# Four chained graph networks: edge ranks by units of 32 columns, and the empty slots filled ahead of the small loads

## The chip, the cores and the metric

The kernel runs on one core of one Trainium2 chip. The metric is the device time of one execution, in microseconds; of before there are three runs, and their median counts. Engines are named as in the profile: PE is TensorE (PEld its weight loads), DVE is VectorE, ACT is ScalarE, POOL is GpSimd, SP is SyncE, which here only issues DMAs.

## The reference, cut to what matters

Four graph networks run one after the other on the same graph of 6,250 nodes with 64 features and 200,000 edges (src, dst, a weight, 16 and 8 attributes). Each one reads rows of its node table at src, works on them, and sums them by dst:

```python
edge_index = jnp.stack([src, dst])
h = jnp.maximum(_layernorm(x, axis=-1), 0.0)
x = x + _L0_gnn_ref(h, L0_gnn_W, L0_gnn_b, edge_weight, src, dst)      # 3 layers: segment_sum(w * ht[col], row)
h = jnp.maximum(_layernorm(x, axis=-1), 0.0)
x = x + _L1_gnn_ref(h, edge_attr_16, ..., src, dst)                    # attention, softmax by dst
h = jnp.maximum(_layernorm(x, axis=-1), 0.0)
x = x + _L2_gnn_ref(h, edge_index, edge_attr_8, ...)                   # MLP on edges, segment_sum by dst
h = jnp.maximum(_layernorm(x, axis=-1), 0.0)
x = x + _L3_gnn_ref(h, src, dst, ...)                                  # attention, softmax by dst
```

The change touches none of these sums, but the sort of the edges that stands ahead of them.

## The kernel before, in words

The nodes are cut into 49 tiles of 128 (T), and the kernel first sorts the edges by the tile of their dst. There are NB = 50 bins, one per tile and one for padding. The edges lie as 128 partitions by KC = 1568 columns. The sort has these steps:

1. SP loads the constants and dst. DVE writes a template of empty slots into `fill`, and SP stores it 42 times (640 KB each) over `packed`, the table of sorted records in DRAM, so that slots which get no edge are harmless. Ahead of these stores SP issues 40 small loads of weights (`small_loads`), the group ids and X.
2. DVE and ACT count the edges of each bin per partition (`bucket` holds each edge's bin); PE makes prefix sums, and DVE turns them into `base`, the place of the first edge of each bin and partition, less one. DVE also makes a schedule of tiles, `sched_i`, which SP stores to DRAM and loads back.
3. DVE ranks the edges. For a group of columns and each bin it makes a mask, a running count that starts at `base`, the new carry, the count where the mask is one, and adds that to `rank`: five instructions per bin and group. The groups are `PLACED`, 2, 3, 5, 9, 15 and 15 units of 32 columns. After each group `rank` becomes the slot number `pos`, and `pos_made` is raised.
4. SP loads the edges' records (`slab`, from `payload`) and their positions (`slab_pos`) by halves of a unit, 16 columns each, into one of two buffers, when `pos_made` covers the group and the scatters that read the buffer have landed (`scattered`).
5. POOL scatters the records, one indirect DMA per column, 32 a unit and 1568 in all, to `packed`. It starts when all 42 fills have landed (`filled`), since they write the same table.

When the last scatter has landed, SP loads the sorted records piece by piece (UZ<-packed), DVE unpacks them, and the passes over the edges begin: gathers of table rows on POOL, one-hot matrices on DVE, sums on PE. While POOL scatters, DVE goes on after the ranks with work that doesn't need the records: `RES`, which marks the first group of each tile, the small weights, and the node work of the first layer (`layer_input`, `norm_to`, on X and U, which is half of UZ).

The helpers `tt`, `ts`, `stt` and `reduce64` wait for the engine's last instruction and issue tensor_tensor, tensor_scalar, scalar_tensor_tensor and a sum over the last axis. In the profile they appear under one line each, 481, 485, 489 and 477. Names that end in a digit lose it there: EA is EA8, in which bucket, rank, pos and others lie.

Of the kernel before, what the change touches and what calls it, by code (L numbers as in the profile page):

```python
# [19 lines left out]
ALU = mybir.AluOpType  # L20
# [3 lines left out]
P = 128  # L24
# [7 lines left out]
NB = T + 1  # L32
KC = -(-N_EDGES // (P * 32)) * 32
SLAB = 16
# [1 line left out]
BODY = 16  # L36
LAG = 8
NG = -(-((N_EDGES + T * (GE - 1)) // GE) // BODY) * BODY
PLACED = [2, 3, 5, 9, 15, 15]
ACT_BINS = 28  # L40
PACK = 40
NS = 1680
# [19 lines left out]
LN_EPS = 1e-5  # L62

assert STEPS_N % 2 == 1 and 2 * ITER * PIECE == 2 * NG
assert max(PLACED) * 2 * SLAB <= 512 and sum(PLACED) * 2 * SLAB == KC and NS % PACK == 0 and (NS // PACK) % 2 == 0 and KC % (2 * SLAB) == 0
assert NS * P >= NG * GE + P * KC - N_EDGES + GE and P * SCHED >= NG + BODY

# [32 lines left out]
def build(nc, d, out):  # L101
    with ExitStack() as ctx:
        def sb(name, shape, dt=F32):
            return ctx.enter_context(nc.sbuf_tensor(name, shape, dt))

        def sem(name):
            return ctx.enter_context(nc.semaphore(name))
# [3 lines left out]
        UZ = sb("UZ", [P, 2, TP, D])  # L111
# [15 lines left out]
        bucket, mask, signs, rank = (ea8_flat[:, i * KC:(i + 1) * KC] for i in range(4))  # L127
        signs = signs.bitcast(BF16).rearrange("p (h c) -> p h c", h=2)
        dst_raw = ea8_flat[:, 5 * KC:6 * KC].bitcast(I32)
        pos = ea8_flat[:, 6 * KC:7 * KC].bitcast(I32)  # L130
        pos_hi = ea8_flat[:, 7 * KC:8 * KC].bitcast(I32)
# [8 lines left out]
        fill = y_flat[:, 0:PACK * PAY].rearrange("p (s c) -> p s c", c=PAY)  # L140
        slab = y_flat[:, PACK * PAY:PACK * PAY + 2 * SLAB * PAY].rearrange("p (h s c) -> p h s c", h=2, c=PAY)
        slab_pos = sb("slab_pos", [P, 2, SLAB], I32)
        itmp = sb("itmp", [P, 2, PIECE], I32)
        prod16 = sb("prod16", [P, PIECE, D16])
        cnt, base, tot, grp, cum = (sb(n, [P, NB]) for n in ("cnt", "base", "tot", "grp", "cum"))
# [6 lines left out]

        const = sb("const", [P, C_ALL])
        ident, tri = const[:, C_ID:C_ID + P], const[:, C_TRI:C_TRI + P]
        iota, ones = const[:, C_IOTA:C_IOTA + P], const[:, C_ONE:C_ONE + P]
        bins, groups = const[:, C_BIN:C_BIN + NB], const[:, C_GRP:C_GRP + SCHED]
        pad_nodes = const[:, C_PAD:C_PAD + PAD_TILES]
# [72 lines left out]
        bank = [ctx.enter_context(nc.psum_tensor(f"bank{i}", [P, 512], F32)) for i in range(8)]  # L230
# [10 lines left out]
        packed = nc.dram_tensor("packed", (P, NS, PAY), F32).ap()  # L241
# [7 lines left out]
        fill_made, filled = sem("fill_made"), sem("filled")  # L249
# [1 line left out]
        counted, prefixes = sem("counted"), sem("prefixes")  # L251
        bucket_made, signs_summed = sem("bucket_made"), sem("signs_summed")
        sched_made, sched_stored, sched_loaded = sem("sched_made"), sem("sched_stored"), sem("sched_loaded")
        pos_made = sem("pos_made")
        slab_in = [sem("slab_in0"), sem("slab_in1")]
        scattered = [sem("scattered0"), sem("scattered1")]
        pack_in = [sem("pack_in0"), sem("pack_in1")]
# [53 lines left out]
        def ds(start, size):  # L311
            return slice(start, start + size) if isinstance(start, int) else bass.ds(start, size)
# [5 lines left out]
        def _(sp):  # L318
# [8 lines left out]
            for h in range(2):  # L327
                at = slice(h * D, (h + 1) * D)
# [7 lines left out]
                for k in range(h * D8, P, 2 * D8):  # L336
                    small_loads.append((we_f[k:k + D8, h, :], d["w2_1"][2 * D:2 * D + D8, :]))

            sp.wait_ge(fill_made, 1)
            for to, what in small_loads:  # L340
                sp.dma_start(to, what).then_inc(s_w, 16)
            sp.dma_start(gid, d["group_ids"]).then_inc(s_gid, 16)
            sp.dma_start(X[:, 0:T, :], d["x"]).then_inc(s_x, 16)

            sp.wait_ge(fill_made, 2)
            for k in range(NS // PACK):
                sp.dma_start(packed[:, k * PACK:(k + 1) * PACK, :], fill).then_inc(filled, 16)

            sp.wait_ge(sched_made, 2)
            sp.dma_start(sched_d.rearrange("(p j) -> p j", p=P), sched_i[:, :]).then_inc(sched_stored, 16)  # L350
# [4 lines left out]
            for h in range(2):  # L355
                sp.dma_start(slab[:, h, :, :], d["payload"][:, h * SLAB:(h + 1) * SLAB, :]).then_inc(slab_in[h], 16)
                sp.dma_start(slab_pos[:, h, :], pos[:, h * SLAB:(h + 1) * SLAB]).then_inc(slab_in[h], 16)
            for j in range(len(PLACED)):
                sp.wait_ge(pos_made, j + 1)
                with sp.Fori(max(sum(PLACED[:j]), 1), sum(PLACED[:j + 1])) as i:  # L360
                    for h in range(2):
                        sp.wait_ge(scattered[h], i * (16 * SLAB))
                        at = i * (2 * SLAB) + h * SLAB
                        sp.dma_start(slab[:, h, :, :], d["payload"][:, bass.ds(at, SLAB), :]).then_inc(slab_in[h], 16)
                        sp.dma_start(slab_pos[:, h, :], pos[:, bass.ds(at, SLAB)]).then_inc(slab_in[h], 16)

            for h in range(2):
                sp.wait_ge(scattered[h], KC // (2 * SLAB) * 16 * SLAB)
# [84 lines left out]
        def _(v):  # L453
            own = Own(v, dve_done)
# [20 lines left out]
            def reduce64(to, what):  # L475
                own.wait()
                own.count(v.tensor_reduce(to, what, AX.X, ALU.add))

            def tt(to, a, b, op):
                own.wait()  # L480
                own.count(v.tensor_tensor(to, a, b, op))

            def ts(to, a, s1, s2, op0, op1=ALU.bypass):
                own.wait()
                own.count(v.tensor_scalar(to, a, s1, s2, op0, op1))

            def stt(to, a, s, b, op0, op1):
                own.wait()
                own.count(v.scalar_tensor_tensor(to, a, s, b, op0, op1))
# [5 lines left out]
            def move(to, a):  # L495

                return v.tensor_scalar(to, a, 1.0, None, ALU.mult)  # L497
# [13 lines left out]
            v.memset(fill[:, :, DST_AT:DST_AT + 1].bitcast(I32), NO_DST).then_inc(fill_made, 1)  # L511
            own.count(v.memset(X[:, T:TP, :], 0.0))
            own.count(v.memset(sched[:, :], 0))
            own.count(v.memset(SRC[:, 2 * NG:], 0))
            own.count(v.memset(rank, 0.0))
            own.count(v.tensor_copy(iota_b[:, :], iota))
            own.count(v.tensor_copy(ident_b[:, :], ident))

# [8 lines left out]
            at0 = own.n  # L527
# [32 lines left out]
            v.memset(itmp[:, :, :], 0).then_inc(sched_made, 1)  # L560

            c1 = 0
            for units in PLACED:
                c0, c1 = c1, c1 + units * 2 * SLAB
                here = slice(c0, c1)
                ps_mask, ps_scan = bank[3][:, 0:c1 - c0], bank[4][:, 0:c1 - c0]
                at0 = own.n
                with v.Fori(0, NB) as b:
                    own.n = b * 5 + at0  # L570
                    one, carry = bins[:, bass.ds(b, 1)], base[:, bass.ds(b, 1)]
                    ts(ps_mask, bucket[:, here], one, None, ALU.is_equal)
                    own.wait()
                    own.count(v.tensor_tensor_scan(ps_scan, ones[:, 0:1].to_broadcast([P, c1 - c0]), ps_mask,
                                                   carry, ALU.mult, ALU.add))
                    own.wait()
                    own.count(move(carry, ps_scan[:, c1 - c0 - 1:c1 - c0]))
                    stt(ps_mask, bucket[:, here], one, ps_scan, ALU.is_equal, ALU.mult)
                    tt(rank[:, here], rank[:, here], ps_mask, ALU.add)
                own.n = at0 + 5 * NB  # L580
                own.wait()
                own.count(v.tensor_copy(pos[:, here], rank[:, here]))
                own.wait()
                own.count(v.tensor_scalar(pos_hi[:, here], pos[:, here], 7, None, ALU.logical_shift_right))
                own.wait()
                own.count(v.tensor_scalar(pos[:, here], pos[:, here], P - 1, None, ALU.bitwise_and))
                own.wait()
                v.scalar_tensor_tensor(pos[:, here], pos[:, here], float(NS), pos_hi[:, here],
                                       ALU.mult, ALU.add).then_inc(pos_made, 1)

            own.count(v.memset(RES[:, :], 0.0))
# [1 line left out]
            at0 = own.n  # L594
# [12 lines left out]
            for h in range(2):  # L607
                at = slice(h * D, (h + 1) * D)
# [12 lines left out]
            for k in range(3):  # L621
                at = slice(32 * k, 32 * k + 32)
                own.count(v.tensor_copy(WE[at, :], we_parts[at, k, :]))
            at = slice(96, P)
# [1052 lines left out]
```

## Time and profile before

| what | before |
| --- | --- |
| runs, us | 14564.51, 14566.06, 14582.17 |
| median | 14566.06 us |
| the profiled execution's own time | 14585.36 us |
| its span from first to last instruction | 14583.5 us |
| PE, DVE, POOL, ACT busy | 9509.5, 10155.7, 10612.6, 4114.1 us |
| first and last scatter of the sort, start | 157.3 and 2198.1 us |

Engines work side by side, so these busy times overlap. The first 2,200 us are the sort, and the rest the six passes over the edges. "Start" counts from the span's first instruction.

### The profile page before, as it was taken

To read this page: it belongs to the slowest core of one execution; us is meant where nothing else is said; L and a number is where in the kernel's file an instruction comes from. 1 tells how busy PE (TensorE), PEld (TensorE's weight loads), DVE (VectorE), ACT (ScalarE), POOL (GpSimd) and SP (SyncE) were. 2 spreads that over 40 slices of the span, in tenths; PEclk is the share of its full clock that TensorE was granted. 3 is DMA by queue.
4 is the path that set the end of the run, shared out by engine and by line. 5 is a ranking of instruction groups with operands and counts; after the bars stand their busy time and mean duration, and the time that the engine had idled before them with its cause. 6 is when DMAs were issued, how large, how long until landed. Compare 5 with 4: busy or idle time off the path is not lost.

```text
span 14583.5 us, 379790 instructions
## 1 busy us (share of the span) xinstructions
PE 9509.5 (65%) x89162; PEld 8547.0 (59%) x89163; DVE 10155.7 (70%) x46548; ACT 4114.1 (28%) x13780; POOL 10612.6 (73%) x10932
## 2 busy tenths in 40 slices
PE   0000006777778888788887888887555555788888
PEld 0000006777767777677776777777444444777777
DVE  7870007777776666666666888888766666888888
ACT  1000000000000000000000888887222222677777
POOL 3777777777767777677776777776677777677776
PEclk9995558888888888888888555555555555555555
DMA  2101112222211111111111111111111111111111
GB/s 100 27 25 26 26 26 48 41 42 41 38 27 26 27 27 27 27 27 27 27 27 26 28 28 27 27 27 23 28 26 26 27 27 26 28 27 27 27 27 29
DMA packets 499490, 443.36 MB, mean 30 GB/s; under 512 B 291533, under 2 KB 316749, under 8 KB 498254
## 3 DMA queue, kind: packets, MB, share of 16 engines
q0 software_dynamic: 349696, 337.89, 14.0%
q1 hardware_dynamic: 149454, 102.38, 2.5%
q14 instruction: 303, 2.48, 0.1%
q8 instruction: 37, 0.61, 0.0%
HBM read 368.39 MB, written 65.20 MB: 30 GB/s over the span
## 4 chain that ended last, share of the span: by engine, by line
PE 35%; issue 18%; DVE 17%; POOL 15%; DVEq 8%; DMA 6%; ACT 1%; POOLq 0%; ACTq 0%; SPq 0%
PE bank L1463 16%; PE bank L1438 11%; POOL packed L423 10%; POOL G L442 6%; DMA G<-table,idx 5%; DVEq L705 3%; PE bank L1520 3%; DVE OH L722 2%; PE bank L1532 2%; PE bank L1451 1%; PE bank L1509 1%; DVE OHB L733 1%; DVEq L707 1%; DVE OHT L761 1%; PE bank L1536 1%
## 5 line engine op out<-in xcount | busy, mean ns | idle before, releaser
L442 POOL DMA_INDIRECT G<-table,idx x9360 | 9084.3, 971 | 3264.8 <-issue 2412.9
L1463 PE MATMUL bank<-UZ,OHT 128*128 128x192 bf16 x15600 | 2086.4, 260 | 544.8 <-DVE OHT L761 544.8
L1438 PE MATMUL bank<-G,OH 128*128 128x64 f32 x9984 | 1686.3, 301 | 598.1 <-DVE OH L722 454.9
L423 POOL DMA_INDIRECT packed<-Y,slab_pos x1568 | 1528.1, 975 | 670.5 <-issue 494.7
L1356 ACT ACTIVATE OHB<-bank,const 128x512 bf16<-128x512 f32 x159 | 109.3, 688 | 6729.7 <-PE bank L1451 6729.7
L1463 PE MATMUL bank<-UZ,V 128*128 128x192 bf16 x14976 | 1992.8, 259 | 0.0
L1438 PEld LDWEIGHTS bank<-G,OH 128*128 128x128 f32 x9984 | 1496.1, 217 | 772.2 <-DVE OH L722 693.9
L1463 PEld LDWEIGHTS bank<-UZ,OHT 128*128 128x128 bf16 x15600 | 1505.8, 111 | 584.6 <-DVE OHT L761 563.1
L1438 PE MATMUL bank<-ZR,OH 128*128 128x65 f32 x6656 | 1765.6, 419 | 1.3 <-DVE ZR L829 1.3
L1438 PEld LDWEIGHTS bank<-ZR,OH 128*128 128x128 f32 x6656 | 1623.9, 334 | 1.9 <-DVE ZR L829 1.7
L722 DVE TENSOR_SCALAR OH<-const,DL,W 128x128 f32<-128x128 f32 x4992 | 1561.2, 368 | 0.2 <-issue 0.2
L761 DVE TENSOR_SCALAR OHT<-OHB 128x512 bf16<-128x512 bf16 x3900 | 1161.4, 298 | 388.5 <-issue 387.2
L866 DVE TENSOR_TENSOR ACC<-ACC,bank 128x64 f32 x2496 | 550.8, 221 | 1248.8 <-PE bank L1438 1206.3
L1463 PEld LDWEIGHTS bank<-UZ,V 128*128 128x128 bf16 x14976 | 1404.6, 104 | 16.0
L1532 PE MATMUL bank<-ER,OHT 128*128 x9984 | 959.8, 174 | 454.9 <-DVE negm_lo L807 265.9
L1520 PE MATMUL bank<-const,V 128*128 128x128 f32 x3328 | 1119.7, 440 | 147.4 <-ACT V L1322 145.4
L1532 PEld LDWEIGHTS bank<-ER,OHT 128*128 128x128 bf16 x9984 | 801.4, 109 | 702.8 <-issue 554.3
L761 DVE TENSOR_SCALAR V<-OHB 128x512 bf16<-128x512 bf16 x3744 | 1136.5, 304 | 0.0
L1451 PE MATMUL bank<-const,chosen 128*128 128x128 f32 x1272 | 220.8, 328 | 1297.6 <-DVE chosen L497 1297.6
L733 DVE TENSOR_TENSOR OHB<-iota_b,DLw 128x256 bf16<-128x256 bf16 x2496 | 1051.5, 421 | 21.3 <-issue 13.5
L1509 PE MATMUL bank<-ident_b,OHB 128*128 128x128 bf16 x4992 | 1009.3, 306 | 43.4 <-DVE OHB L733 43.4
L1451 PEld LDWEIGHTS bank<-const,chosen 128*128 128x128 f32 x1272 | 193.7, 231 | 1298.2 <-DVE chosen L497 1298.2
(281 smaller groups left out, 18632.0 us busy)
## 6 DMA issues: line engine op xcount, KB each, us to landing
G<-table,idx POOLq DMA_INDIRECT x9360, 2.5
packed<-Y SPq DMA_DIRECT2D x42, 640.0 KB, 17.4
UZ<-packed SPq DMA_DIRECT2D x104, 256.0 KB, 2.7
Y<-in_payload SPq DMA_DIRECT2D x98, 256.0 KB
packed<-Y,slab_pos POOLq DMA_INDIRECT x1568
table<-Y SPq DMA_DIRECT2D x6, 1690.0 KB, 5.5
idx<-SRC SPq DMA_DIRECT2D x624, 8.0 KB
X<-in_x SPq DMA_DIRECT2D x1, 1568.0 KB, 8.8
```

The costliest lines, as they stand in the source:

```text
L423: pool.indirect_dma_start(out=packed_rows, out_offset=bass.IndirectOffsetOnAxis(ap=slab_pos[:, h, c:c + 1], axis=0), in_=slab[:, h, c, :], ...
L442: pool.indirect_dma_start(out=G[:, 2 * q + c, :], out_offset=None, in_=table, in_offset=bass.IndirectOffsetOnAxis(ap=idx[:, h, j:j + 1], a ...
L722: o = v.tensor_scalar(OH[:, q, c, :], iota, DL[:, at], W[:, at], ALU.is_equal, ALU.mult)
L733: v.tensor_tensor(OHB[:, q, :, :], iota_b[:, :].unsqueeze(1).to_broadcast([P, 2, P]), DLw[:, 2 * u:2 * u + 2].unsqueeze(2).to_broadcast([P ...
L761: v.tensor_scalar(tile_hot(tile), code, float(tile), None, ALU.is_equal).then_inc(tile_ready, 1)
L866: v.tensor_tensor(acc, acc, ps_a[r % 2][:, 0:D], ALU.add).then_inc(acc_done, 1)
L1438: o = pe.matmul(ps_a[r % 2][:, 0:w], OH[:, q, c, :], parts[c], start=c == 0, stop=c == 1)
L1451: o = pe.matmul(ps_code[:, c * P:(c + 1) * P], chosen[:, c:c + 1].to_broadcast([P, P]), ident, start=True, stop=True)
L1463: o = pe.matmul(ps_rows[c // 2][:, c % 2 * 3 * D:(c % 2 + 1) * 3 * D], tile_hot(tile)[:, c * P:(c + 1) * P], table_parts[:, tile, :, :].re ...
L1509: o = pe.matmul(ps_m[r % 2][:, c * P:(c + 1) * P], OHB[:, q, c, :], ident_b[:, :], start=True, stop=True)
L1520: o = pe.transpose(ps_x[r % 2][:, c * P:(c + 1) * P], V[:, r % 4, c, :], ident)
L1532: pe.matmul(e[:, c:c + 1], one, ER3[:, bass.ds(t, 1), k], start=k == 0, stop=k == 2)
```

## The change

The ranks are no longer made bin by bin over groups of columns, but unit by unit over all bins at once. For the 32 columns of a unit, `in_bin` (50 bins by 32 columns) holds a one where an edge is in a bin; `from_base`, its product with `base`, summed over the bins, gives each edge its base; `as_mine` (32 by 32) marks pairs of columns with the same bin, and times `not_later` it counts the edges of the same bin up to this one. `in_unit`, the sum over the columns of in_bin, moves `base` on to the next unit. The scratch lies in UZ, which holds nothing yet. `pos_made` now tells of the first unit and `pos_next` of each further one, and SP waits for it once per unit. `rank` and its clearing go. On SP the 42 fills now stand ahead of the small loads, the ids and X, and wait for the finished template at once.

```diff
-PLACED = [2, 3, 5, 9, 15, 15]
+UNIT = 32
+UNITS = KC // UNIT
+PLACE_OPS = 11
...
+        rank_unit, in_unit = sb("rank_unit", [P, 2, UNIT]), sb("in_unit", [P, NB])
+        work = UZ[:, :, :, :].rearrange("p h t c -> p (h t c)")
...
-            sp.wait_ge(fill_made, 1)
+            sp.wait_ge(fill_made, 2)
+            for k in range(NS // PACK):
+                sp.dma_start(packed[:, k * PACK:(k + 1) * PACK, :], fill).then_inc(filled, 16)
+
             for to, what in small_loads:
                 sp.dma_start(to, what).then_inc(s_w, 16)
             sp.dma_start(gid, d["group_ids"]).then_inc(s_gid, 16)
             sp.dma_start(X[:, 0:T, :], d["x"]).then_inc(s_x, 16)
 
-            sp.wait_ge(fill_made, 2)
-            for k in range(NS // PACK):
-                sp.dma_start(packed[:, k * PACK:(k + 1) * PACK, :], fill).then_inc(filled, 16)
-
...
-            for j in range(len(PLACED)):
-                sp.wait_ge(pos_made, j + 1)
-                with sp.Fori(max(sum(PLACED[:j]), 1), sum(PLACED[:j + 1])) as i:
...
+            with sp.Fori(1, UNITS) as i:
+                sp.wait_ge(pos_next, i * (16 * SLAB))
+                for h in range(2):
+                    sp.wait_ge(scattered[h], i * (16 * SLAB))
+                    at = i * (2 * SLAB) + h * SLAB
+                    sp.dma_start(slab[:, h, :, :], d["payload"][:, bass.ds(at, SLAB), :]).then_inc(slab_in[h], 16)
+                    sp.dma_start(slab_pos[:, h, :], pos[:, bass.ds(at, SLAB)]).then_inc(slab_in[h], 16)
...
+            own.count(v.tensor_tensor(not_later, iota[:, 0:UNIT].unsqueeze(1).to_broadcast([P, UNIT, UNIT]),
+                                      iota[:, 0:UNIT].unsqueeze(2).to_broadcast([P, UNIT, UNIT]), ALU.is_le))
             own.count(v.memset(SRC[:, 2 * NG:], 0))
-            own.count(v.memset(rank, 0.0))
...
+            def place(i):
+
+                here = ds(i * UNIT, UNIT)
+                mine = bucket[:, here]
+                per_bin = [P, NB, UNIT]
+                tt(in_bin, mine.unsqueeze(1).to_broadcast(per_bin), bins.unsqueeze(2).to_broadcast(per_bin), ALU.is_equal)
+                tt(as_mine, mine.unsqueeze(1).to_broadcast([P, UNIT, UNIT]), mine.unsqueeze(2).to_broadcast([P, UNIT, UNIT]),
+                   ALU.is_equal)
+                tt(from_base, in_bin, base[:, :].unsqueeze(2).to_broadcast(per_bin), ALU.mult)
+                tt(as_mine, as_mine, not_later, ALU.mult)
+                reduce64(in_unit[:, :], in_bin)
+                reduce64(rank_unit[:, 0, :], from_base.rearrange("p b c -> p c b"))
+                reduce64(rank_unit[:, 1, :], as_mine)
+                tt(base[:, :], base[:, :], in_unit[:, :], ALU.add)
+                tt(pos[:, here], rank_unit[:, 0, :], rank_unit[:, 1, :], ALU.add)
...
+            place(0).then_inc(pos_made, 1)
+            v.wait_ge(pos_made, 1)
+            at0, each = own.n, PLACE_OPS
+            with v.Fori(1, UNITS) as i:
+                own.n = i * each + (at0 - each)
+                place(i).then_inc(pos_next, 16 * SLAB)
```

In what follows L... is a line of the kernel it is from, and names in brackets behind "waits" are semaphores. On DVE, in place of the loop over bins (here for the first group, one turn of 50, in which bank is PSUM and EA holds bucket and rank), before:

```order
L569 ISA
L485 ISA [waits dve_done]
L485 TENSOR_SCALAR bank<-EA,const 128x64
L84 REGISTER_ALU
L574 ISA [waits dve_done]
L574 SCALAR_TENSOR_TENSOR bank<-const,base,bank 128x64
L84 REGISTER_ALU
L497 TENSOR_SCALAR base<-bank 128x1 [waits dve_done]
L84 REGISTER_ALU
L489 SCALAR_TENSOR_TENSOR bank<-EA,const,bank 128x64 [waits dve_done]
L84 REGISTER_ALU
L481 TENSOR_TENSOR EA<-EA,bank 128x64 [waits dve_done]
```

now stands this, once for each unit (here the one ahead of the loop, which has the same twelve; UZ holds the scratch):

```order
L487 TENSOR_TENSOR UZ<-EA,const 128x1600 [waits dve_done]
L487 TENSOR_TENSOR UZ<-EA 128x1024 [waits dve_done]
L487 TENSOR_TENSOR UZ<-UZ,base 128x1600 [waits dve_done]
L487 TENSOR_TENSOR UZ<-UZ 128x1024 [waits dve_done]
L483 TENSOR_REDUCE in_unit<-UZ 128x50 [waits dve_done]
L483 TENSOR_REDUCE rank_unit<-UZ 128x32 [waits dve_done] x2
L487 TENSOR_TENSOR base<-base,in_unit 128x50 [waits dve_done]
L487 TENSOR_TENSOR EA<-rank_unit 128x32 [waits dve_done]
L586 TENSOR_SCALAR EA<-EA 128x32 [waits dve_done]
L588 TENSOR_SCALAR EA<-EA 128x32 [waits dve_done]
L590 SCALAR_TENSOR_TENSOR EA<-EA 128x32 [waits dve_done]
```

Five short instructions for each of 50 bins, with one operand or the output in PSUM, have become twelve for 32 columns and all bins, and the first four read two operands from SBUF.

On SP, the queue between the load of dst and the load of the first records, before:

```order
L321 DMA EA<-in_dst 128x1568
L341 DMA rows<-in_rows_b 128x576 [waits fill_made]
...
L342 DMA V<-in_group_ids 128x832
L343 DMA X<-in_x 128x3136
L347 DMA packed<-Y 128x1280 [waits fill_made]
L347 DMA packed<-Y 128x1280 x41
L350 DMA sched_d<-sched_i 128x7 [waits sched_made]
L352 DMA sched<-sched_d 1x896 [waits sched_stored]
L356 DMA Y<-in_payload 128x512 [waits pos_made]
```

and now:

```order
L329 DMA EA<-in_dst 128x1568
L349 DMA packed<-Y 128x1280 [waits fill_made]
L349 DMA packed<-Y 128x1280 x41
L352 DMA rows<-in_rows_b 128x576
...
L353 DMA V<-in_group_ids 128x832
L354 DMA X<-in_x 128x3136
L357 DMA sched_d<-sched_i 128x7 [waits sched_made]
L359 DMA sched<-sched_d 1x896 [waits sched_stored]
L363 DMA Y<-in_payload 128x512 [waits pos_made]
```

The fills (packed<-Y) moved past 42 loads, and the store and the load of the schedule now stand directly behind X; the rest keeps its order.

## Rows read from the trace of the kernel before

**Rows 1.** The page, part 1: busy time, share, instructions of each engine.

```profile
PE 9509.5 (65%) x89162; PEld 8547.0 (59%) x89163; DVE 10155.7 (70%) x46548; ACT 4114.1 (28%) x13780; POOL 10612.6 (73%) x10932
```

**Rows 2.** The chain of waits, 0 to 3000 us: start, us, what.

```profile
2198.09 2.13 DMA packed<-Y,slab_pos
2200.28 2.81 DMA UZ<-packed
```

**Rows 3.** Who waited for whom, 0 to 2700 us: total, times, longest.

```profile
DVE W L497 <- DMA UZ<-packed: 1155.5, 4, 1153.1
POOL packed L423 <- DMA slab_pos<-EA: 175.8, 3, 156.8
```

**Rows 4.** POOL's scatters, line 423: min/median/max ns, first and last start.

```profile
L423 POOL DMA_INDIRECT packed<-Y,slab_pos x1568: 955/962/5448, 157.3 to 2198.1; - x196
```

**Rows 5.** Timeline of POOL: start us, us, instruction, idle before and its releaser.

```profile
157.31 1.12 POOL L423 DMA_INDIRECT packed<-Y,slab_pos  x1 [156.85 <-DMA slab_pos<-EA]
...
237.18 0.96 POOL L423 DMA_INDIRECT packed<-Y,slab_pos  x1 [0.30 <-issue]
256.81 0.96 POOL L423 DMA_INDIRECT packed<-Y,slab_pos  x1 [18.68 <-DMA slab_pos<-EA]
```

**Rows 6.** Timeline of DVE at the end of the first rank group.

```profile
150.77 0.29 DVE L485 TENSOR_SCALAR bank<-EA,const 128x64 f32<-128x64 f32 x1 [0.26 <-DVE EA L481]
151.19 0.35 DVE L574 TENSOR_TENSOR_SCAN bank<-const,base,bank 128x64 f32<-128x64 f32 x1
...
153.22 0.23 DVE L588 SCALAR_TENSOR_TENSOR EA<-EA 128x64 int32<-128x64 int32 x1
```

**Rows 7.** Timeline of SP's queue (time to issue), 0 to 160 us.

```profile
3.62 0.33 SPq L341 DMA_DIRECT2D rows<-in_rows_b  x1
...
25.28 59.16 SPq L347 DMA_DIRECT2D packed<-Y  x42
84.48 1.35 SPq L350 DMA_DIRECT2D sched_d<-sched_i  x1
...
100.58 0.23 SPq L352 DMA_DIRECT2D sched<-sched_d  x1
153.47 0.35 SPq L356 DMA_DIRECT2D Y<-in_payload  x1
```

**Rows 8.** Busy time by stretch: PE, PEld, DVE, ACT, POOL, clock, DMA, GB/s.

```profile
90.00:100.00 10.00, 0.00 (x0) 0.00 (x0) 7.17 (x28) 0.00 (x0) 0.00 (x0) 1.00 0.77 314
100.00:150.00 50.00, 0.00 (x0) 0.00 (x0) 36.19 (x139) 0.00 (x0) 0.00 (x0) 1.00 0.00 0
```

**Rows 9.** Groups of DVE by shape: busy us, mean ns, idle before.

```profile
L481 DVE TENSOR_TENSOR UZ<-UZ 128x3328 f32<-128x3328 f32 x2 | 7.3, 3626 | 0.1
L477 DVE TENSOR_REDUCE n_a<-X 128x52 f32<-128x3328 f32 x1 | 3.6, 3619 | 0.0
L481 DVE TENSOR_TENSOR UZ<-cum,const 128x343 f32<-128x343 f32 x1 | 0.5, 516 | 0.0
L477 DVE TENSOR_REDUCE sched_f<-UZ 128x7 f32<-128x343 f32 x1 | 0.5, 510 | 0.0
```

**Rows 10.** Timeline of DVE: the last write of the template of empty slots.

```profile
4.20 0.09 DVE L511 MEMSET Y<- 128x40 int32 x1
```

**Rows 11.** DMA issues: KB each, us from issue to landing.

```profile
X<-in_x SPq DMA_DIRECT2D x1, 1568.0 KB, 8.8
```

**Rows 12.** Timeline of DVE and POOL, 978 to 987 us.

```profile
978.20 3.62 DVE L481 TENSOR_TENSOR UZ<-X,n_a 128x3328 f32<-128x3328 f32 x1
978.79 3.88 POOL L423 DMA_INDIRECT packed<-Y,slab_pos  x1 [0.31 <-issue]
981.86 3.62 DVE L481 TENSOR_TENSOR UZ<-UZ 128x3328 f32<-128x3328 f32 x1
982.97 3.35 POOL L423 DMA_INDIRECT packed<-Y,slab_pos  x1 [0.30 <-issue]
985.52 3.62 DVE L477 TENSOR_REDUCE n_arg<-UZ 128x52 f32<-128x3328 f32 x1
986.62 0.96 POOL L423 DMA_INDIRECT packed<-Y,slab_pos  x1 [0.30 <-issue]
```

**Rows 13.** Groups of DVE by shape, 60 to 1000 us: the steps on RES.

```profile
L489 DVE SCALAR_TENSOR_TENSOR RES<-V,cum,RES 128x832 f32<-128x832 f32 x49 | 55.1, 1124 | 6.6
```

More of the change, by code:

```diff
@@ L64 @@
 assert STEPS_N % 2 == 1 and 2 * ITER * PIECE == 2 * NG
-assert max(PLACED) * 2 * SLAB <= 512 and sum(PLACED) * 2 * SLAB == KC and NS % PACK == 0 and (NS // PACK) % 2 == 0 and KC % (2 * SLAB) == 0
+assert UNIT == 2 * SLAB and UNITS * UNIT == KC and NS % PACK == 0 and (NS // PACK) % 2 == 0 and KC % (2 * SLAB) == 0
 assert NS * P >= NG * GE + P * KC - N_EDGES + GE and P * SCHED >= NG + BODY
@@ L154, in build @@
         ident, tri = const[:, C_ID:C_ID + P], const[:, C_TRI:C_TRI + P]
+        rank_unit, in_unit = sb("rank_unit", [P, 2, UNIT]), sb("in_unit", [P, NB])
+        work = UZ[:, :, :, :].rearrange("p h t c -> p (h t c)")
+        tiles_wide = NB * UNIT
+        in_bin, from_base = (work[:, k * tiles_wide:(k + 1) * tiles_wide].rearrange("p (b c) -> p b c", c=UNIT) for k in range(2))
+        as_mine, not_later = (work[:, 2 * tiles_wide + k * UNIT * UNIT:2 * tiles_wide + (k + 1) * UNIT * UNIT].rearrange(
+            "p (a c) -> p a c", c=UNIT) for k in range(2))
         iota, ones = const[:, C_IOTA:C_IOTA + P], const[:, C_ONE:C_ONE + P]
@@ L253, in build @@
         sched_made, sched_stored, sched_loaded = sem("sched_made"), sem("sched_stored"), sem("sched_loaded")
-        pos_made = sem("pos_made")
+        pos_made, pos_next = sem("pos_made"), sem("pos_next")
         slab_in = [sem("slab_in0"), sem("slab_in1")]
@@ L357, in _ @@
                 sp.dma_start(slab_pos[:, h, :], pos[:, h * SLAB:(h + 1) * SLAB]).then_inc(slab_in[h], 16)
-            for j in range(len(PLACED)):
-                sp.wait_ge(pos_made, j + 1)
-                with sp.Fori(max(sum(PLACED[:j]), 1), sum(PLACED[:j + 1])) as i:
[L361 to L365, printed above, removed]
+            with sp.Fori(1, UNITS) as i:
[5 more added lines that the diff above has]
+                    sp.dma_start(slab_pos[:, h, :], pos[:, bass.ds(at, SLAB)]).then_inc(slab_in[h], 16)
             for h in range(2):
@@ L560, in _ @@
             v.memset(itmp[:, :, :], 0).then_inc(sched_made, 1)
[L563 to L582, printed above, removed]
+            def place(i):
[12 more added lines that the diff above has]
+                tt(pos[:, here], rank_unit[:, 0, :], rank_unit[:, 1, :], ALU.add)
                 own.wait()
@@ L587, in _ @@
                 own.wait()
-                v.scalar_tensor_tensor(pos[:, here], pos[:, here], float(NS), pos_hi[:, here],
-                                       ALU.mult, ALU.add).then_inc(pos_made, 1)
+                return v.scalar_tensor_tensor(pos[:, here], pos[:, here], float(NS), pos_hi[:, here], ALU.mult, ALU.add)
+            place(0).then_inc(pos_made, 1)
[4 more added lines that the diff above has]
+                place(i).then_inc(pos_next, 16 * SLAB)
+            own.n = at0 + each * (UNITS - 1)
+            v.wait_ge(pos_next, (UNITS - 1) * 16 * SLAB)
             own.count(v.memset(RES[:, :], 0.0))
```

## The prediction

> **What bounds the kernel now.** The page gives shares over the whole program, and no engine fills it (POOL 73%, DVE 70%) [rows 1]; the change lies in the first 2,200 us, so I read that stretch. The chain of waits there shows what ends it: the last record scatter is issued at 2198.09 us, and the first read of the sorted records starts at 2200.28, as soon as it has landed [rows 2]. The list of waits says that the others have been ready for long: DVE waits 1153.1 us for those reads [rows 3]. So until 2198 us the bound is POOL, which issues 1568 scatters of 0.962 us (median) [rows 4], each with 0.30 us of idle time ahead of it [rows 5]; their starts lie 1.265 us apart. Back to back they would need 1567 x 1.265 = 1982 us. The stretch from 157.31 to 2198.09 has 2041 us, so some 59 us are stalls, and there are 157 us ahead of it.
>
> Two waits can be won. The timeline of POOL shows its first scatter at 157.31, held by the load of the positions, and a second hold of 18.68 us at 256.81 [rows 5], where the second group of positions was not ready. What made them late stands in two timelines. DVE issues five instructions per bin at some 1.8 us, 50 bins for the first 64 columns, and ends at 153.45; the payload load is issued at 153.47 and the first scatter starts 3.84 us later [rows 6, 7]. SP's queue was done much earlier: the 42 fills of the empty slots are issued from 25.28 to 84.44, the store behind them at 84.48 has landed by 100.58, and the DMA engines stand still from 100 us [rows 7, 8]. Their share is 0.77 of 90 to 100 us, so the last fill lands near 97.5. Ranks alone cost the last 50 us.
>
> **The change, part by part.** *Ranks of one unit.* From the pair of rows for 343 and 3328 elements, a two-input f32 operation in SBUF costs 516 ns, and 3625 - 516 over 2985 elements makes 1.0415 ns for each further one; the reduction has the same slope, 510 and 3619 ns [rows 9]. That gives 1.825 us for 1600 elements and 1.225 for 1024, in TENSOR_TENSOR, and 1.819 and 1.219 in TENSOR_REDUCE. A unit has two and two of the first kind (6.10 us), two and one of the second (4.86), and five small ones of 32 or 50 columns, which I put at 0.94 together: 0.17 to 0.21 each, since a 64-wide one takes 0.23 [rows 6] and 32 elements fewer are 0.03. Between dependent instructions lie 0.035 us, 0.13 before one that takes a register in its address, and 0.26 to 0.28 at a loop's start [rows 6]: 0.87 in all. One unit: 12.78 us. Not shown is a reduction that reads at a stride of 32 elements, as the one of from_base does. Bounds: the same as a dense one, or twice it (14.6 us a unit); I take the first, since nothing in the rows of broadcast operands shows a price for the access.
>
> Unit 0 is then ready at 61.9 + 12.8 = 75 us, unit i at 75 + 12.8 i. POOL takes 32 x 1.265 = 40.5 us for a unit, so the waits on pos_next, one per unit where there were six, are met far ahead; the hold of 18.4 us (18.68 less the usual 0.30) goes. DVE is done with ranks near 688 us. What follows on it (the 49 steps on RES, the node work, X and the small weights) has over 1,100 us of cover [rows 3].
>
> *Order on SP.* The fills are issued from 4.3 us, when the last write of their template ends [rows 10], instead of 25.28. Their issue took 59.2 us, with X and the group ids in front of them; so it ends at 59 to 63.5. Behind come 40 small loads, ids and X, 21.7 us of issue before (3.62 to 25.28) [rows 7], to 81 or 85; then the store of the schedule. That one took 16 us to land behind a queue of fills; now only X (1568 KB, 8.8 us to landing [rows 11]) is in front, so it lands about 89 to 94. The payload's issue follows, and 3.84 us later the first scatter: 93 to 98 us, I take 95. The fills, 13 us behind their issue as before (97.5 - 84.4), land near 75. DVE's unit 0 is ready at 75. So neither of them is last any more; SP's own issue is. Gain at the head: 157.3 - 95 = 62.3 us. Bounds: 88 (small loads go out freely and the store lands in a few us) and 105 (small loads held until the fills have drained, then 21.7 us, the store and the loads). The clear of rank goes (1.36 us by its 1568 elements) and not_later comes (1.2 us): nothing.
>
> *What the new DVE work does to POOL.* This is the price. The timeline of DVE and POOL at 978 us shows it: the scatter that starts at 978.79, during a TENSOR_TENSOR that runs from 978.20 to 981.83 with both inputs in SBUF, takes 3.88 us in place of 0.96, and ends 0.84 after that instruction; the next one takes 3.35 and ends 0.83 after the next TENSOR_TENSOR. During the TENSOR_REDUCE at 985.52 scatters take 0.96 again [rows 12]. The old loop had one input or the output in PSUM (bank), and the median scatter shows no such cost [rows 4, 6]. All four big TENSOR_TENSOR of a unit have both inputs in SBUF. The rows also show that a blocked scatter slips through in the 0.035 us between two of them.
>
> So per unit: the scatter caught by the first one ends 0.84 after its end; the next starts 0.30 later, and finds the 1.225 one finished (1.26 - 1.14 = 0.12 us after its start, where a free one would begin its reading); the next is caught by the second 1.825 one for some 0.6 us; the next passes at the end of the fourth. Then six or so run free until the next unit. By rows, nine scatters fit between one unit and the next, and what is lost is 12.78 - 9 x 1.267 = 1.38 us (ten would need 12.67 plus the blocked 0.6, which doesn't fit). From 95 to 688 us are 46.4 units: 46.4 x 1.38 = 64 us. Bounds by the same count: 46 us with a unit of 12.4, 98 with one of 13.5, where the tenth just misses; 85 to 90 for the strided one at double price.
>
> In the Trainium skill, SBUF — State Buffer, section "Who interferes with whom", two sentences bear on this and pull apart: an instruction of DVE with two SBUF inputs contends with a GpSimd instruction that reads SBUF, yet in the page's probe tensor_tensor did not stall DMAs, which it explains (as inferred) by descriptor generation needing only the write side. By the second, the sum would be -81 us. The row agrees with the first: this scatter reads its positions from SBUF.
>
> **Sum.** -62.3 (head) - 18.4 (second hold) + 64 (blocked scatters) = -16.7 us, a shift of all that follows 2198 us, which is not changed. The profiled execution had 14585.36 us (span 14583.5), so 14568.7 in its terms; it lies 19.3 above the median of the runs shown, 14566.06, from which I go: **14549 us**, -0.12%. A measurement of this kernel can tell some 0.2% (29 us) from no change.
>
> **Rivals.**
> 1. *No contention* for TENSOR_TENSOR of this size: -62.3 - 18.4 = -81, 14485 us. For it: the 49 steps on RES also have two inputs in SBUF and take 1.12 us each [rows 13], and the scatters beside them show 0.96; but with their idle time those steps come 1.26 us apart, the scatters' own pitch, so each can find the gap. Against: both scatters beside a long TENSOR_TENSOR, one of them with a broadcast input (n_a) [rows 12]. Chance 0.1.
> 2. *The burst closes POOL off*: if a waiting scatter doesn't get in between the four instructions, it loses the 6.2 us of them. Then some six scatters fit in a unit: 12.78 - 6 x 1.267 = 5.2 us lost, x 46.4 = 240 us; -81 + 240 = +159, 14725 us, slower. It decides from 2.4 us lost per unit on (110 in all). Against: at 981.83 the blocked scatter got through in 0.03 us. Chance 0.06, with 0.03 for losses of 110 to 240 by some pattern between.
> 3. *Gain at the head smaller and units dearer*: first scatter at 105 (-52), loss 90: -52 - 18 + 90 = +20, 14586 us, no change. For it: SP's queue was full while fills were under way (59 us for 42 issues). Chance 0.2.
> The forecast has the remaining 0.61, with its own range of 14525 (first scatter at 88, loss 46) to 14570.
>
> **How the numbers follow.** Faster by over 0.2% (below 14537) are rival 1 and about a quarter of the forecast: 0.26. Slower by over 0.2% (over 14595) is rival 2 with its neighbours: 0.09. Within: 0.65. The range leaves out rivals 1 and 2 and reaches from the low end of the forecast to rival 3: 14520 to 14588.
>
> **What would show it.** First scatter at 93 to 98 and no hold of 18 us behind it; DVE's unit at 12.4 to 13.5 us; scatters of 1.2 to 2.4 us during the TENSOR_TENSOR of every unit up to 690 us, nine or so starts per unit; from then on 1.265 us apart; the last scatter near 2181 in place of 2198. Wrong it would be with scatters of 0.96 throughout (rival 1) or of 6 us (rival 2), with the first one beyond 105, or with a unit over 40 us, when POOL would wait for DVE.

## The result, and the profile after

The changed kernel took 14586.31 us (median of 22 runs, 14578.93 to 14594.8); the kernel before, run beside it on the same chip, 14563.33 us (22 runs). The ratio is 1.0016, with an interval of 1.0009 to 1.0022: some 23 us slower, where 14549 and a small gain stood in the forecast. The profiled execution has a span of 14592.7 us.

The sort did what the prediction said. POOL's scatters, to be read against [rows 4]. This row gives their busy us, the mean ns of one, and what ended the idle time before them:

```profile
L429 POOL DMA_INDIRECT packed<-Y,slab_pos x1568 | 1590.1, 1014 | 593.1 <-issue 495.6 <-DMA slab_pos<-EA 97.5
```

The wait for slab_pos is 97.5 us in one piece, where it was 175.8 in three [rows 3]: the first scatter starts at 97.98 and there is no second hold. The same row of before has 1528.1 us busy; so 62.0 us have come in as longer scatters. Where, a timeline of DVE and POOL over one unit shows (start, us):

```profile
102.75 1.82 DVE L487 TENSOR_TENSOR UZ<-EA,const 128x1600 f32<-128x1600 f32 x1 [0.42 <-issue]
103.21 2.20 POOL L429 DMA_INDIRECT packed<-Y,slab_pos  x1 [0.30 <-issue]
104.61 1.22 DVE L487 TENSOR_TENSOR UZ<-EA 128x1024 f32 x1
105.71 0.96 POOL L429 DMA_INDIRECT packed<-Y,slab_pos  x1 [0.30 <-issue]
105.87 1.82 DVE L487 TENSOR_TENSOR UZ<-UZ,base 128x1600 f32<-128x1600 f32 x1
106.97 1.55 POOL L429 DMA_INDIRECT packed<-Y,slab_pos  x1 [0.30 <-issue]
107.73 1.23 DVE L487 TENSOR_TENSOR UZ<-UZ 128x1024 f32<-128x1024 f32 x1
108.83 0.96 POOL L429 DMA_INDIRECT packed<-Y,slab_pos  x1 [0.31 <-issue]
108.99 1.82 DVE L483 TENSOR_REDUCE in_unit<-UZ 128x50 f32<-128x1600 f32 x1
110.09 0.96 POOL L429 DMA_INDIRECT packed<-Y,slab_pos  x1 [0.30 <-issue]
...
116.79 1.82 DVE L487 TENSOR_TENSOR UZ<-EA,const 128x1600 f32<-128x1600 f32 x1 [0.41 <-issue]
```

Two scatters are caught, and take 2.20 and 1.55 us in place of 0.96; the others slip past. A unit takes 116.79 - 102.75 = 14.04 us. The chain of waits then shows the end of the sort, 15.4 us earlier than in [rows 2]:

```profile
2182.71 2.11 DMA packed<-Y,slab_pos
2184.87 2.75 DMA UZ<-packed
```

What the prediction left out comes later. Each pass over the edges begins with the store of its table. The table below goes from store to store in the two profiled executions, in us. A turn is one round of a pass's loop on DVE; the turn given is that of the fourth pass.

| stretch | before | after | difference |
| --- | --- | --- | --- |
| start to first store | 2218.5 | 2202.5 | -16.0 |
| pass 1 (sums) | 1928.2 | 1918.7 | -9.5 |
| passes 2 and 3 (sums) | 3860.6 | 3858.1 | -2.5 |
| pass 4 (attention) | 2241.1 | 2278.4 | +37.3 |
| its turn | 41.31 | 42.11 | +0.80 |
| pass 5 (MLP) | 2189.9 | 2183.2 | -6.7 |
| pass 6 (attention) | 2145.3 | 2152.0 | +6.7 |

The differences add up to 9.2 us, which is what lies between the two profiled spans. The medians lie 23 us apart, since the profiled execution of before was 22 us above its median and that of after 8. So the table shows where time went, and only to some 14 us how much of the 23. Passes 5 and 6 differ by no more than the profiled runs 1 to 4 and 8 to 11 below do among themselves (2183 to 2193 us and 2137 to 2156), so nothing is read from them.

The two stores that bound pass 4 stand in SP's timeline of after, and the same two of before at 8007.28 and 10248.37:

```profile
7979.15 0.32 SPq L389 DMA_DIRECT2D table<-Y  x1
10257.58 0.33 SPq L389 DMA_DIRECT2D table<-Y  x1
```

The diff touches no instruction of that pass. The list of waits over 1000 us of it (24 turns; total us, times, longest), 8507 to 9507 us of before:

```profile
PE bank L1532 <- DVE negm_lo L807: 87.3, 95, 3.0
DVE DLw L497 <- issue: 19.5, 25, 0.8
```

and 8479 to 9479 us of after:

```profile
PE bank L1542 <- DVE negm_lo L817: 107.1, 95, 3.9
DVE DLw L503 <- issue: 36.1, 24, 1.8
```

Ahead of DLw, once a turn, DVE stands 0.7 us longer on "issue", that is, idle without a wait that the profile shows. (The issue time ahead of another instruction, r_negm, falls from 17.0 to 5.5 us in the same stretch.) PE waits 0.8 us a turn longer for DVE. The page's table of DMA queues (packets, MB, share) has one row that differs, the queue that brings code. Before, then after:

```profile
q14 instruction: 303, 2.48, 0.1%
```

```profile
q14 instruction: 553, 4.53, 0.1%
```

The trace also shows where in a turn the time goes. Put side by side instruction by instruction, as a mean over the turns of pass 4, DVE makes four pauses in each turn, of some 0.36 us beyond what the same step takes without one, behind instructions 17, 145, 273 and 401 of the loop before, and 89, 217, 345 and 473 after: moved by exactly 72, and as many and as long in both. What differs is the branch back to the loop's start. From the branch to the next instruction DVE takes 0.54 us before and 1.31 after, and this 0.77 us is nearly the whole 0.80 of the turn. The last pause lies 88 instructions ahead of the loop's end before, and 16 after. (These means are worked out from the trace's own instructions and stand in no row.)

### The profile page after: what moved, and what is told of

Its sections match the earlier page's. It is cut to its first block, busy times and chain, and to the rows that moved or that the text cites. A ratio compares the mean times of both kernels' runs of the same rounds, so it can differ in the third digit from the quotient of the medians.

```text
span 14592.7 us, 377063 instructions
## 1 busy us (share of the span) xinstructions
PE 9533.0 (65%) x89162; PEld 8575.3 (59%) x89163; DVE 10109.2 (69%) x45612; ACT 4127.9 (28%) x13780; POOL 10668.1 (73%) x10932
## 4 chain that ended last, share of the span: by engine, by line
PE 31%; issue 20%; DVE 18%; POOL 16%; DVEq 8%; DMA 5%; SPq 1%; ACT 0%; POOLq 0%; ACTq 0%
PE bank L1473 16%; POOL packed L429 11%; PE bank L1448 10%; POOL G L448 6%; DMA G<-table,idx 5%; DVEq L715 3%; DVE OH L732 2%; PE bank L1530 2%; PE bank L1542 1%; DVE OHB L743 1%; PE bank L1461 1%; DVE ZR L839 1%; DVEq L717 1%; DVEq L86 1%; DVE OHT L771 1%
## 5 line engine op out<-in xcount | busy, mean ns | idle before, releaser
L429 POOL DMA_INDIRECT packed<-Y,slab_pos x1568 | 1590.1, 1014 | 593.1 <-issue 495.6
```

Of the source, the lines that this page charges most:

```text
L429: pool.indirect_dma_start(out=packed_rows, out_offset=bass.IndirectOffsetOnAxis(ap=slab_pos[:, h, c:c + 1], axis=0), in_=slab[:, h, c, :], ...
```

## The experiments

The theory: the later code has moved against the blocks in which it is fetched, and pass 4 pays for that. Its rival: something of the sort itself (where the scratch or UZ lies, the order of loads, the earlier start of all that follows) slows pass 4. Runs 1 to 4 shared a chip on which the kernel before takes 14563 us, runs 8 to 11 one on which it takes 14590. Runs 5 to 7 fell on a third, where it takes 19707. Each ratio is to the kernel before on the same chip. The filler instructions below are memsets of one unused column; they run where DVE has over 1,100 us to spare.

**Run 1.** The changed kernel with 72 one-column memsets on DVE ahead of `memset(RES)`, so that the code behind has its old place:

```diff
+            for _ in range(72):
+                own.wait()
+                own.count(v.memset(pad[:, :], 0.0))
             own.count(v.memset(RES[:, :], 0.0))
```

> The changed kernel with 72 one-column memsets of an unused tile put on DVE behind the ranks, where DVE has over 1,200 us to spare, so that all of DVE's later instructions stand at the same places of its program as before the change (3590 instructions as before, the changed kernel has 3518). Theory A, code position: the loop of the first attention pass (fetches of 8 KB of DVE's code, five a turn) goes back from 42.10 us a turn to 41.29, and the second one's fetches (5 a turn, none before) vanish; the passes take what they took before, and only the sort's gain of 15 us is left: ratio to before 0.999, near 14548 us. Theory B, the lost time comes from the shift in time itself (clock, DMA) or from SP: the turn stays at 42.1 us and the ratio at 1.0016.

14547.86 us, ratio 0.999 (0.9981 to 0.9999). Pass 4 takes 2239.8 us with a turn of 41.29, as before the change, pass 1 takes 1927.1, and code packets are 302 (303 before the change). Seventy-two instructions more make the changed kernel 38 us faster.

**Run 2.** The other way round: the kernel before with 56 memsets there, which puts the later code at the same place in a block of 128 as after the change (72 fewer and 56 more differ by 128).

> The kernel before with 56 such memsets on DVE behind its ranks. 56 and the -72 of the change are the same shift modulo 128 instructions (8 KB). Theory A: the first attention pass takes 42.1 us a turn, the second one fetches code five times a turn, and the kernel is slower by 38 to 45 us, ratio 1.0028, though nothing of the change is in it. Theory B: ratio 1.000, turns of 41.29 us. The sort is unchanged in both (last scatter near 2198 us).

14599.07 us, ratio 1.0023 (1.0014 to 1.0032), 36 us over the kernel before. Pass 4 takes 2277.8 us with a turn of 42.1, its packets come at instructions 9, 100, 225, 356 and 482 of the loop, and pass 1 takes 1917.9. The page's row of the code queue:

```profile
q14 instruction: 555, 4.55, 0.1%
```

The whole loss, and the small gain of pass 1, appear with no part of the change in the kernel, so the rival falls.

**Run 3.** Does a second operand in PSUM free the scatters? `base`, the bins, a copy of the unit's buckets, and not_later go to PSUM banks, so that each large tensor_tensor reads one operand from SBUF and one from PSUM; the fillers are 64 (3590 instructions again).

```diff
+        not_later = [bank[k][:, :].rearrange("p (a c) -> p a c", c=UNIT) for k in (4, 5)]
+        base_p, bins_p, mine_p = bank[3][:, 0:NB], bank[3][:, 64:64 + NB], bank[3][:, 128:128 + UNIT]
...
-                tt(in_bin, mine.unsqueeze(1).to_broadcast(per_bin), bins.unsqueeze(2).to_broadcast(per_bin), ALU.is_equal)
+                own.count(v.tensor_copy(mine_p, mine))
+                tt(in_bin, mine.unsqueeze(1).to_broadcast(per_bin), bins_p.unsqueeze(2).to_broadcast(per_bin), ALU.is_equal)
...
-                tt(from_base, in_bin, base[:, :].unsqueeze(2).to_broadcast(per_bin), ALU.mult)
+                tt(from_base, in_bin, base_p.unsqueeze(2).to_broadcast(per_bin), ALU.mult)
```

> The changed kernel with base, a copy of the bins, a copy of the unit's bins and not_later in PSUM, so that none of the big TENSOR_TENSOR of a unit reads two operands from SBUF (three more small instructions a unit), and 64 fillers, which makes 3590 instructions again. Theory A1, two SBUF operands block the scatters: scatters take 0.96 us during the ranks too, the last one starts 64 us earlier than in the changed kernel, near 2119 us, and the ratio to before is 0.9945 (near 14484 us), or 0.997 if code position plays no part. Rival: scatters are blocked by long DVE work of any kind, or by writes to UZ: their median and the last start (2183 us) stay.

14489.99 us, ratio 0.9949 (0.9935 to 0.9962), 58 us under run 1. DVE and POOL over the same stretch:

```profile
104.27 3.08 DVE L490 TENSOR_TENSOR UZ<-EA,bank 128x1600 f32<-128x1600 f32 x2
104.47 0.96 POOL L432 DMA_INDIRECT packed<-Y,slab_pos  x1 [0.30 <-issue]
105.74 0.95 POOL L432 DMA_INDIRECT packed<-Y,slab_pos  x1 [0.30 <-issue]
107.00 0.96 POOL L432 DMA_INDIRECT packed<-Y,slab_pos  x1 [0.30 <-issue]
107.38 3.26 DVE L490 TENSOR_TENSOR UZ<-UZ,bank 128x1600 f32<-128x1600 f32 x3
108.26 0.96 POOL L432 DMA_INDIRECT packed<-Y,slab_pos  x1 [0.31 <-issue]
109.52 0.96 POOL L432 DMA_INDIRECT packed<-Y,slab_pos  x1 [0.30 <-issue]
```

and the groups of DVE and POOL:

```profile
L490 DVE TENSOR_TENSOR UZ<-EA,bank 128x1600 f32<-128x1600 f32 x49 | 89.2, 1821 | 1.7
L490 DVE TENSOR_TENSOR UZ<-UZ,bank 128x1600 f32<-128x1600 f32 x49 | 89.2, 1820 | 1.7
L432 POOL DMA_INDIRECT packed<-Y,slab_pos x1568 | 1522.7, 971 | 593.6 <-issue 496.1 <-DMA slab_pos<-EA 97.5
```

The instructions take as long as with both operands in SBUF and still write UZ, and no scatter is held; so neither their length nor their output was what held them. The scatters' busy time falls from 1588.5 us (run 1) to 1522.7, and the last one starts at 2115.85 instead of 2181.4. So the second SBUF operand costs 66 us of the sort here, and 58 of the time.

**Run 4.** Is there a better place for the loop than the one before the change? With 95 fillers (3613 instructions) the four pauses above move 95 instructions towards the loop's start, from 89, 217, 345 and 473. The first then falls ahead of the loop, and its 489 instructions should lie within four blocks, 4 x 128 = 512.

> The changed kernel with 95 fillers in place of 72. The loop of the first attention pass has 489 instructions. In the traces a fetch starts at its instructions 28, 156, 282, 411 before and 100, 228, 356, 484 after. If DVE keeps four blocks of 128 and the loop lies within four, as this shift should make it, theory A expects no fetch in that pass, and turns below 41.29 us, near 40.6; the second attention pass may fetch (0.12 us a turn). Ratio to before 0.997. If only the distance of the last fetch from the loop's end counts, five fetches a turn stay, and the turn is about 41.3. Theory B: 42.1 us, ratio 1.0016.

14518.79 us, ratio 0.9968 (0.9956 to 0.998). Pass 4 takes 2201.2 us with a turn of 40.51. From 7985 to 10180 us 9 code packets come:

```profile
q14 instruction: 9, 0.07, 0.0%
```

and in its list of waits (8485 to 9485 us) both rows of above have shrunk:

```profile
PE bank L1546 <- DVE negm_lo L821: 67.6, 24, 2.9
DVE DLw L504 <- issue: 12.4, 24, 0.5
```

The four pauses are gone, and the branch back takes 0.27 us. The same pass thus turns in 40.51, 41.29 or 42.10 us by where its code lies: no refetch, and refetch at two alignments. Pass 6, which the expectation had down for a possible refetch, has 9 packets.

**Runs 5 and 11: the order of loads alone** in the kernel before.

```diff
+            sp.wait_ge(fill_made, 2)
+            for k in range(NS // PACK):
+                sp.dma_start(packed[:, k * PACK:(k + 1) * PACK, :], fill).then_inc(filled, 16)
-            sp.wait_ge(fill_made, 1)
             for to, what in small_loads:
```

> The kernel before with only the new order on SP: the 42 fills ahead of the small loads, ids and X. DVE's program is unchanged. Theory: the ranks of the first 64 columns end at 153.4 us and still hold the first scatter, so the order alone is worth nothing: first scatter near 157, last near 2198, ratio 1.000. Rival, the fills or the queue held it: first scatter earlier than 150 us.

> The fifth run's kernel again: the kernel before with the fills ahead of the small loads and nothing else. The first scatter waits for the ranks of the first records, not for the queue: first scatter at 157, time as before within 0.1% (14563 us, ratio 1.000). Rival: the small loads, which now issue later and slower, come late for the first steps that need them; then 10 to 25 us more.

Run 5: 19717.99 us on the third chip, ratio 1.0009 (0.9999 to 1.0019). Run 11: 14589.19 us, ratio 1.0 (0.9991 to 1.001). The first scatter starts at 157.45 and 157.2 us, so the new order alone is worth nothing. The schedule is back early and the records wait for the ranks, as SP's timeline of run 11 shows:

```profile
93.90 0.24 SPq L351 DMA_DIRECT2D sched<-sched_d  x1
153.36 0.34 SPq L355 DMA_DIRECT2D Y<-in_payload  x1
```

**Runs 6 and 10: the ranks alone**, the changed kernel with SP's old order and 72 fillers.

> The changed kernel with SP's old order, and 72 fillers for the old code position. Theory: the store of the schedule lands near 100.6 us behind the fills as before, the records' load follows, and the first scatter starts near 104.5 in place of 98 (new order) or 157 (before); the last near 2188; some 10 us less than before, ratio 0.9993, against 0.999 with both parts. So the ranks bring nearly all of the earlier start, and the order 6 to 7 us. Rival: without the new order the fills hold the scatters beyond 110 us.

> The sixth run's kernel again: the changed ranks, the queue's order of before, 72 fillers so that the later code lies as in the kernel before. First scatter at 103 to 105 us, last scatter near 2187 us, time 14553 us (ratio 0.9993): some 5 us above the first run, which is what the changed order of loads is worth beside the changed ranks. Rival: the order of loads was worth the small-load stretch (26 us); then first scatter at 124 and 14574 us.

Run 6: 19408.19 us on the third chip, ratio 0.9853 (0.9839 to 0.9868). Run 10: 14576.99 us, ratio 0.9993 (0.9983 to 1.0002). The first scatter starts at 103.34 and 103.26 us, where run 1 has 98.18. So the new order of loads is worth 5.1 us at the head once the ranks are quick, which the time cannot tell from nothing.

**Run 8: runs 3 and 4 together** (one operand in PSUM, 87 fillers, 3613 instructions).

> The changed kernel with one operand of each large rank step in PSUM (as in the third run) and 87 fillers instead of 64, so that the loop of the first attention pass lies within four blocks of 128 instructions (as in the fourth run). It computes the whole reference. On a chip that runs the kernel before in 14563 us: the third run gave 14490, and the fourth stood 29 us below the first; if the two add up, this one takes 14461 us (ratio 0.993), with the last scatter near 2116 us, 0.96 us for each scatter, and a turn of the first attention pass at 40.5 us with about a dozen code fetches. Rival: the gain of the fourth run was not from the place of the loop in the blocks but from the place of something else; then a turn stays at 41.3 and the time at 14490.

14486.45 us, ratio 0.9928 (0.9911 to 0.9944), with a turn of 40.56, 51 code packets in the whole program, and the last scatter at 2120.89. The two gains add up: it is 103 us under the kernel before, where run 3 had 73 and run 4 stood 29 below run 1.

**Runs 7 and 9: the records first.** Run 8 with the first records ahead of the small loads:

```diff
             for h in range(2):
                 sp.dma_start(slab[:, h, :, :], d["payload"][:, h * SLAB:(h + 1) * SLAB, :]).then_inc(slab_in[h], 16)
                 sp.dma_start(slab_pos[:, h, :], pos[:, h * SLAB:(h + 1) * SLAB]).then_inc(slab_in[h], 16)
+            for to, what in small_loads:
+                sp.dma_start(to, what).then_inc(s_w, 16)
```

> A version from the findings: the changed kernel with base, bins and not_later in PSUM (as in e3), on SP the schedule and the records of the first unit ahead of the small loads, ids and X, and 87 fillers, which puts DVE's loops where e4 had them (3613 instructions). Expected: the first scatter near 79 us, when rank unit 0 is ready (74.5) and the fills have landed, against 98; POOL without stalls from there, last scatter near 2097; the first attention pass at 40.5 us a turn without fetches. Against e3 (14490): 19 us at the head and 29 to 38 us in the pass, so 14433 to 14442 us, ratio 0.991. Rival: the small loads on SP (some 22 us of issue) delay the records of unit 1 and POOL waits for them at its 17th scatter, which gives part of the 19 us back.

> The same kernel as the seventh run, now meant for a chip that runs the kernel before in 14563 us: one operand in PSUM, four blocks, and the load of the first records put ahead of the small loads. First scatter at 79 us instead of 98, one late refill of 3.4 us as seen there, last scatter near 2100 us, time 14445 us (ratio 0.992): 16 us below the version that has the small loads first. Rival: the table of the first pass or its edges now wait for what the small loads bring; then the passes begin no earlier and it takes 14461.

Run 7: 19464.24 us on the third chip, ratio 0.9881 (0.9864 to 0.9898), with the first scatter at 78.83. Its last came only at 2250.13, because the scatters themselves take longer there: 1646.1 us in all against 1528.4 in run 8, with one wait of 3.4 us for records. Run 9: 14460.05 us, ratio 0.991 (0.9894 to 0.9927), first scatter at 79.0, last at 2101.39, 19.5 us ahead of run 8's. The late refill that was expected didn't come, and the first store of a table moved with the scatters, from 2140.7 to 2121.3, so nothing in pass 1 was held up by the later small loads. This is the best version: 130 us under the kernel before on its chip.

## Why the prediction was wrong, step by step

- **The step that failed** is the last half of a sentence of the sum: "a shift of all that follows 2198 us, which is not changed". The sum put the passes at nothing. Their instructions were not changed, but their place in the code was, by 72 instructions, and for that pass 4 took 37.3 us more and pass 1 took 9.5 less. Runs 1 and 2 show it from both sides. With the place kept (run 1) the kernel takes 14547.86 us, where the forecast had 14549.
- **Head**: 62.3 us forecast, 59.3 measured (157.31 - 97.98). The fills are issued from 4.21 in 52.83 us, not 59; but the first ten small loads took 1.37 us each, up to 71 us, and those behind them 0.60 (before, with the fills behind them, all took 0.60). The DMA engines were full until some 72 us and nearly idle from 75, so the slow ones were issued while the fills drained:

```profile
4.21 52.83 SPq L349 DMA_DIRECT2D packed<-Y  x42
57.08 1.37 SPq L352 DMA_DIRECT2D rows<-in_rows_b  x1
...
73.31 0.60 SPq L352 DMA_DIRECT2D RW<-in_w  x1
...
87.56 0.42 SPq L357 DMA_DIRECT2D sched_d<-sched_i  x1
93.94 0.24 SPq L359 DMA_DIRECT2D sched<-sched_d  x1
```

- **Second hold**: 18.4 us, gone as forecast; POOL waits once for positions.
- **A unit** was 14.04 us, not 12.78. The strided reduction, for which I took the price of a dense one, costs 1.55 times it, 1.00 us more; the rest of the sum is 0.26 us short:

```profile
L483 DVE TENSOR_REDUCE rank_unit<-UZ 128x32 f32<-128x1600 f32 x49 | 138.2, 2821 | 1.7
L487 DVE TENSOR_TENSOR UZ<-UZ,base 128x1600 f32<-128x1600 f32 x49 | 89.4, 1825 | 1.7
L483 DVE TENSOR_REDUCE in_unit<-UZ 128x50 f32<-128x1600 f32 x49 | 89.2, 1820 | 1.7
```

- **Blocked scatters**: 1.38 us a unit forecast with nine scatters in it. With the longer unit ten fit, and 14.04 - 10 x 1.267 = 1.37 us is lost: the same by luck, since the longer instruction is a reduction, which blocks nothing. 62.0 us measured against 64. Rival 1 (no contention) falls by the timeline above and by run 3; rival 2 (the burst shuts POOL out) falls too, since three scatters end within the burst of 102.75 to 108.96 us, at 105.41, 106.67 and 108.52.
- **The sum for the sort**: -59.3 - 18.4 + 62.0 = -15.7, read 15.4, forecast 16.7.
- Rival 3 gives 14586 us, which is what came out, but not by its mechanism: the first scatter was at 98 and not 105, and the loss 62 and not 90.

The Trainium skill, SBUF — State Buffer, section "Who interferes with whom", was weighed in the prediction: its probe of tensor_tensor, which did not stall DMAs, does not carry over to these scatters; 2.20 and 1.55 us beside 0.96, and run 3's 66 us, decide for its other sentence, on two SBUF inputs.

On code, the Trainium skill, Runtime: NRT & Kernel Launch, section "Instruction fetch mechanics", has most engines hold 512 instructions, filled in blocks of 256 one after another at a cost mostly hidden, and warns that a taken branch to outside what is held stalls.
## What to carry to other kernels

## What the runs showed of the hardware that I had not expected

- Pass 6 turns in 40.6 us with 9 packets (run 1) and with 261 (the changed kernel) alike, because DVE has slack in it. In 13000 to 14000 us of run 1 it waits for PE ahead of r_gm 120 times, 39.3 us in all; in the changed kernel, with its pauses for code, it does so once, for 0.4 us. In pass 4 it is PE that waits for DVE, and there the refetches cost time.
- Pass 1, with hardly a fetch, gained 9.5 us by the same shift (run 2 alone: 10.3), by a way that these runs do not show.
- Chips differ by far more than the change. The kernel before took 14563, 14590 and 19707 us on three chips. On the last, DVE's instructions have their usual lengths, but idle "issue" time of up to 5.9 us stands ahead of them in some stretches of the ranks. The waits of DVE in run 5, 0 to 2700 us, where the first chip has none of this in such a place:

```profile
DVE bank L484 <- issue: 469.0, 118, 5.9
```

Why its instructions come late is open. On that chip the ranks were part of the bound: POOL waits 490.3 us for positions in run 5, and the first store comes at 2627.4 us there and at 2315.5 with the new ranks (run 6). So the ranks were worth 1.5% there, and on the others 0.1% or less.
